# Graph attention, 12 heads: Q and K projected group by group, and stacked by 36 DMAs of 64 KB per batch instead of 12 of 192 KB

## The reference

```python
q = split_heads(x @ Wq + bq); k = split_heads(x @ Wk + bk); v = split_heads(x @ Wv + bv)
scores = q @ k.T / sqrt(32) + beta * adj
scores = where(adj > 0, scores, -9e15)
out = softmax(scores) @ v                 # heads side by side again: 256 x 384
y = layernorm(x + out)                    # over the 384 columns, no affine
```

## Time and profile before

| | us |
|---|---|
| median of 3 runs | 877.06 (875.73 to 879.56) |
| span of the profiled execution | 871.1 |
| PE busy | 748.6 (86%) |
| DVE busy | 643.6 (74%) |
| ACT busy | 632.8 (73%) |
| POOL busy | 420.7 (48%) |
| DMA queue, share of 16 engines | 55.1% |

### The profile page before, as it was taken

How to read it: one execution, slowest core, us unless ns; L and a number is a source line. 1 busy time by engine, 2 the same in 40 slices (tenths; PEclk the granted TensorE clock), 3 DMA queues, 4 the chain that set the end, 5 groups by cost and what they waited for, 6 DMA issues and landing times.

```text
span 871.1 us, 27397 instructions
## 1 busy us (share of the span) xinstructions
PE 748.6 (86%) x6528; PEld 657.1 (75%) x6528; DVE 643.6 (74%) x2487; ACT 632.8 (73%) x2116; POOL 420.7 (48%) x660
## 2 busy tenths in 40 slices
PE   5799998888988888989888989888998888999882
PEld 4678887777887777887777887777787777787761
DVE  3477777777777776877777787777877777787775
ACT  3477877777876777877777877777777777777772
POOL 1312555454555454556454556454456454456453
PEclk9899999999999999999999999999999999999997
DMA  4666444566544566544566545566544566544461
GB/s 151 140 140 140 104 119 117 137 158 155 107 118 114 137 157 156 107 117 116 133 158 157 109 119 116 129 157 158 116 118 114 124 158 157 115 118 113 96 147 36
DMA packets 59226, 111.87 MB, mean 128 GB/s; under 512 B 8704, under 2 KB 34560, under 8 KB 59136
## 3 DMA queue, kind: packets, MB, share of 16 engines
q1 hardware_dynamic: 59136, 111.05, 55.1%
HBM read 22.94 MB, written 12.58 MB: 41 GB/s over the span
## 4 chain that ended last, share of the span: by engine, by line
PE 35%; SPq 33%; DMA 18%; ACT 5%; issue 5%; DVE 3%; ACTq 0%; DVEq 0%
SPq L292 32%; PE j_bank L367 18%; DMA stack<-qk_parts 17%; PE t_bank L396 7%; PE s_bank L381 5%; PE o_bank L412 4%; ACT probs L472 2%; ACT qk_parts L486 2%; DVE qk_parts L567 2%; ACT probs_t L499 1%; PE o_bank L420 1%; DMA beta_col<-in_L_gnn_beta_dram 1%; ACTq L178 0%; PE j_bank L335 0%; DVE w_low L684 0%
## 5 line engine op out<-in xcount | busy, mean ns | idle before, releaser
L472 ACT ACTIVATE probs<-neg_scores,neg_max 128x256 f32<-128x256 f32 x768 | 381.9, 501 | 41.2 <-DVE neg_max L557 37.9
L557 DVE CUSTOM_DVE_ANT_0 neg_scores<-s_bank,bias_sb 128x256 f32<-128x256 f32 x768 | 290.2, 415 | 97.5 <-issue 51.6
L381 PE MATMUL s_bank<-stack 96*128 96x256 f32 x768 | 170.9, 304 | 95.5 <-DMA stack<-qk_parts 95.5
L396 PE MATMUL t_bank<-ident,probs 128*128 128x128 f32 x1536 | 231.4, 272 | 1.8 <-ACT probs L472 1.3
L381 PEld LDWEIGHTS s_bank<-stack 96*128 96x128 f32 x768 | 120.8, 190 | 125.5 <-issue 74.2
L396 PEld LDWEIGHTS t_bank<-ident,probs 128*128 128x128 f32 x1536 | 177.6, 141 | 3.3 <-ACT probs L472 1.8
L486 ACT ACTIVATE qk_parts<-j_bank,qk_bias 128x256 fp32r<-128x256 f32 x192 | 90.7, 473 | 120.6 <-PE j_bank L367 95.6
L577 DVE COPY probs_t<-t_bank 128x512 f32<-128x512 f32 x256 | 175.6, 686 | 1.1 <-PE t_bank L396 1.1
L567 DVE SCALAR_TENSOR_TENSOR qk_parts<-j_bank,qk_bias,qk_parts 128x256 fp32r<-128x256 f32 x192 | 92.4, 481 | 76.4 <-ACT qk_parts L486 76.4
L472 ACT ACTIVATION_READ_ACCUMULATOR probs<-neg_scores,neg_max 128x1 f32 x768 | 146.5, 191 | 0.0
L367 PE MATMUL j_bank<-xt_high,w_high 128*128 128x256 f32 x576 | 116.6, 311 | 6.0 <-ACT w_high L517 5.5
(11 more groups left out here) (59 smaller groups left out, 927.4 us busy)
## 6 DMA issues: line engine op xcount, KB each, us to landing
stack<-qk_parts SPq DMA_DIRECT2D x384, 192.0 KB, 4.0
x_sb<-in_x_dram SPq DMA_DIRECT2D x32, 384.0 KB, 4.9
out_dram<-o_sb SPq DMA_DIRECT2D x31, 384.0 KB, 4.5
adj_sb<-in_adj_dram SPq DMA_DIRECT2D x32, 256.0 KB, 4.8
w_raw<-in_L_gnn_Wq_dram SPq DMA_DIRECT2D x1, 576.0 KB, 4.2
w_raw<-in_L_gnn_Wk_dram SPq DMA_DIRECT2D x1, 576.0 KB, 6.6
w_raw<-in_L_gnn_Wv_dram SPq DMA_DIRECT2D x1, 576.0 KB, 8.2
out_dram<-o_sb SPq DMA_DIRECT2D x2, 192.0 KB, 2.0
```

Source lines behind the costliest of these rows:

```text
L381: mm = pe.matmul(b[:, t * N:(t + 1) * N], stack[0:R, par, 0, j, g, t * P:(t + 1) * P], stack[0:R, par, 1, j, g, :], start=True, stop=True)
L396: mm = pe.transpose(b[:, k * N + t * P:k * N + (t + 1) * P], probs[:, (T * h + t) % (T * NH), k * P:(k + 1) * P], ident[:, :])
L472: nc.scalar.activation(probs[:, slot, :], neg_scores[:, slot, :], ACT.Exp, bias=neg_max[:, par, t, h:h + 1], scale=-1.0, accum_out=row_sum ...
L557: nc.vector.tensor_tensor_reduce(neg_scores[:, (T * h + t) % (T * NH), :], s_bank[h % NS][:, t * N:(t + 1) * N], bias_sb[:, par, t, :], -1 ...
```

## The change

The jobs go Q0 K0 Q1 K1 Q2 K2, so that the two jobs of a group follow each other. `stack_parts` becomes `stack_group`, which moves one group: 12 DMAs of 32 x 2 x 1024 B = 64 KB, each behind a wait for the low part of that group's K job. `stacked` becomes 24 semaphores (parity, group, j) instead of 4, and PE waits at each head for those of that head. In SP's stream group 0 of batch b+1 is issued at the start of batch b, ahead of the loads of x and adj; groups 1 and 2 behind them.

```diff
-    JOB = [(kind, g) for kind in "QK" for g in range(G)] + [("X", 0), ("V", 0), ("X", 1), ("V", 1), ("X", 2)]
+    JOB = [(kind, g) for g in range(G) for kind in "QK"] + [("X", 0), ("V", 0), ("X", 1), ("V", 1), ("X", 2)]
-        stacked = [sem(f"stacked{j}") for j in range(J)]
+        stacked = [[[sem(f"stacked{par}_{g}_{j}") for j in range(J)] for g in range(G)] for par in range(2)]
-            def stack_parts(i, par):
-                multiplied = held(count(i, par, STEPS, -STEPS))
-                wait(sp, low_ready, low_count(i, par, KV - 1))
+            def stack_group(i, par, g):
+                if g == 0:
+                    wait(sp, scores_ready, held(count(i, par, STEPS, -STEPS)))
+                wait(sp, low_ready, low_count(i, par, 2 * g + 1))
                 take_wait(sp, passed_s)
-                wait(sp, scores_ready, multiplied)
                 for j in range(J):
                     for n, (q_part, k_part) in enumerate(PAIRED):
-                        src = qk_parts[HD * j:HD * (j + 1), par, q_part:2 + k_part + 1:2 + k_part - q_part, :, :]
-                        sp.dma_start(stack[HD * n:HD * (n + 1), par, :, j, :, :].bitcast(F32),
-                                     src.bitcast(F32)).then_inc(stacked[j], DMA)
+                        src = qk_parts[HD * j:HD * (j + 1), par, q_part:2 + k_part + 1:2 + k_part - q_part, g, :]
+                        sp.dma_start(stack[HD * n:HD * (n + 1), par, :, j, g, :].bitcast(F32),
+                                     src.bitcast(F32)).then_inc(stacked[par][g][j], DMA)
...
-            stack_parts(0, 0)
+            for g in range(G):
+                stack_group(0, 0, g)
             def batch(i, par):
...
+                if not is_last(i, par):
+                    stack_group(i + par, 1 - par, 0)
                 if not is_tail(i):
...
                     load_adj(i + 1, par)
                 if not is_last(i, par):
-                    stack_parts(i + par, 1 - par)
+                    stack_group(i + par, 1 - par, 1)
+                    stack_group(i + par, 1 - par, 2)
                 if not first:
                     store(i - 1, par)
...
             def scores(i, par, h):
                 g, j = h // J, h % J
-                if g == 0:
-                    wait(pe, stacked[j], count(i, par, PARTS * DMA, PARTS * DMA))
+                wait(pe, stacked[par][g][j], (i + 1) * (PARTS * DMA))
...
             def high(i, par, k):
...
-                    if k == 0:
+                    if q == 0:
                         for j in range(J):
-                            wait(act, stacked[j], count(i, par, PARTS * DMA, -PARTS * DMA))
+                            wait(act, stacked[par][g][j], i * (PARTS * DMA))
```

More of the change, by code:

```diff
@@ L350, in project @@
                 if k < KV:
-                    q, g = k // G, k % G
+                    g, q = k // 2, k % 2
                     pairs = [(wp[:, q, c, g * P:(g + 1) * P], xp[:, par, c, :])
```

## The result

The changed kernel takes 981.54 us in the median (976.61 to 983.27), against 877.07 us for the kernel before: ratio 1.119, with a 95% interval of 1.115 to 1.122. It is slower by 104 us. The forecast was 905 us, slower by 28 us: right in sign, and outside its range of 815 to 935.

A forecast was written before the change was run, and what follows sets the result against it. PE, the busiest engine, was held by waits for stacking DMAs, 2.98 us per batch. Start 53.2, 29 periods of 27.0 (783) and end 63.1 give 899.3, 28.2 over the span; added to 877.06 that is 905 us, range 815 to 935.

The forecast's parts named there:

- the term for the clock: PE behind the late x: granted clock falls in one batch in five, 1.9 us per fall, period 26.6 to 27.0.
- The stack waits go: PE's score matmul: all 2.98 + 0.3 us per batch of waiting for stacking DMAs gone, alone 98 us.
- One 64 KB issue costs 0.64, twelve 7.7: SP's stacking issues: 0.64 us each, so 36 take 23.0 us per batch.
- a cheaper issue: Rival on SP: a 64 KB issue costs 0.43 us, period 24.6, time 826 us; chance 0.22.
- engines held by the number of runs: Rival on the DMA engines: 0.98 us an issue, over 1200 us, or 0.75 and about 1010; chance 0.06.
- SP needs 26.6 us per batch: SP's queue: 23.0 of issues, 3.05 of store and loads, 0.5 of waits.
- x lands 3.65 us after PE wants it: PE at X0: x, issued behind group 0, lands at 386.8 against 383.11; period by this loop 26.5 us.
- the upper bound, 945 us: Clock term on PE: a fall in each batch, period 28.4 us, time 945 us.
- PE without its stack waits needs 22.8 us per batch: PE: period 26.05 less 2.98 of stack waits, less some 0.1 for each of three restarts.
- Start and end: First X0 after the change at 53.2 us with PE at half clock; from the last X0 to the end 63.1 us.
- the first rival: Rival of the cheaper 64 KB issue on SP: X0 of batch 0 at 43.9, 826 us; chance 0.22.
- The limits trade places: Rival: x lands 0.5 us earlier, SP sheds as much, period 26.1, clock holds, 877 us; chance 0.13.

The follow-up runs named there:

- e1: Changed kernel with SP issuing the loads of x and adj ahead of group 0 again, 36 DMAs kept: 873.43 us, ratio 0.995 to the kernel before.
- e3: Changed kernel with groups 1 and 2 stacked in one burst of twelve 128 KB DMAs (24 per batch): 962.24 us, ratio 1.096 to the kernel before.
- e2: Changed kernel with 30 throwaway matmuls on PE ahead of the wait for x: 922.83 us, ratio 1.050 to the kernel before.
- e8: Changed kernel with loads ahead, groups 1 and 2 in one burst, and the loop written out: 766.45 us, ratio 0.873 to the kernel before.
- e5: Changed kernel with the loop written out, no jump back on any engine: 961.78 us, ratio 1.095 to the kernel before.
- e6: Changed kernel with 30 throwaway matmuls ahead of each wait for x and the loop written out: 905.53 us, ratio 1.030 to the kernel before.
- e10: Changed kernel with groups 1 and 2 in one burst, 28 throwaway matmuls and the loop written out: 906.41 us, ratio 1.033 to the kernel before.
- e7: Changed kernel with loads ahead and groups 1 and 2 in one burst, loop kept: 812.70 us, ratio 0.925 to the kernel before.

## Why the prediction was right in sign and too small

The step that failed is the term for the clock: it was to fall in one batch in five, and it fell in every one. A second term was put at nothing without a reason: what DVE does at the jump back, once no stack wait covers it. The rest of the mechanism held.

- *The stack waits go.* Right: none is left.
- *One 64 KB issue costs 0.64, twelve 7.7.* Right: 7.67 to 7.78 in the rows shown. The rivals of a cheaper issue and of engines held by the number of runs are out.
- *SP needs 26.6 us per batch.* Nearly: 26.1 when it is the bound (e1), as store and loads issue in 0.37 to 0.40 each with an undisturbed queue. It was not the bound of the changed kernel (e3).
- *x lands 3.65 us after PE wants it.* Right: 3.84 per batch, landing 3.2 us after its issue. The period that follows, 26.6 with a clock that holds and no jump, is 26.7 in e2. Undoing this one part takes the whole loss back (e1), though there the period is SP's own work, and x is still somewhat late.
- *The granted clock.* Here the term "one batch in five" failed. In the changed kernel it fell behind all 30 waits, and e2 gives the sum: 1.8 us in each batch, against 0.4 taken. That is 1.4 x 29 = 41 us of the 76 that are missing. The price of one fall, 1.9 from the earlier trace rows, was right (the stretch of 30 to 32 us in the earlier trace rows has 0.55 in the mean, where the prediction says 0.50); the upper bound, 945 us, was the better reading. The Trainium skill's rule ("TensorE: Matmul & The Clock Gate", "What's actually happening") said so: the clock follows how busy the array has been, and idling halves it. The trace agrees, with 0.50 to 0.61 behind each wait. The prediction weighed it against the work on both sides of the wait, for which no row stood.
- *PE without its stack waits needs 22.8 us per batch.* Right for PE (e8), wrong for the kernel: it took for granted that nothing hid behind those waits. DVE's gap at each jump back did. The periods give 2.5 us per pass, 1.2 per batch, 35 us in all; together with the clock that is the 76. Written out (e5, e6) only 17 to 20 us of it come back, since the written-out kernels have some half microsecond per batch more on this loop, for a cause that stays open (e10). That e6, with both terms out, measures the 905 us of the forecast is luck: without falls of the clock the forecast was 893.
- *Start and end.* X of batch 2 was issued at 49.5 and forecast at 48.1. From the last X0 to the end it took 66.0 us, forecast 63.1. Both are small beside the 29 periods. Two of the prediction's figures are a little off, without weight in the sum: SP's slack is 12.55 us by its rows, and X0 of the first rival comes out at 43.7.
- *The limits trade places* described e1 (877 forecast, 873 measured), not the changed kernel.

## What to carry to other kernels

Before a step moves ahead in an in-order queue, list what stands behind it and when each of those is wanted; here a load with some 8 us to spare was put behind 7.7 us of issues that had themselves to wait. A wait that goes away uncovers whatever lay beside it, so look for idle time on every engine at the same place, also under the rows marked "issue". And a single long wait of PE can cost more than several short ones of the same sum, since the clock may fall: 2.98 us in three pieces per batch did not bring it down (1.00 from 100 to 850 us of the kernel before), 3.84 in one piece always did, and in e1 single waits from 1.92 us on mostly did.

## What was not expected of the hardware

- Twelve SBUF-to-SBUF DMAs of 64 KB issue at 0.64 us each, the same as twelve of 128 KB (7.77 us in e3), while 192 KB go at 0.95. By the 209 GB/s of the earlier trace rows their bytes would take 0.31, 0.63 and 0.94 us: at 64 KB the issue is the limit, at 192 KB the data, and at 128 KB the two come out alike.
- From its jump back to the first instruction of the next pass DVE's stream takes, in the passes read here, 3.0 us in the changed kernel, 4.2 in the kernel before and 4.4 in e7, and DVE is idle for 2.0 of them in the first and 3.4 in the last; ACT, PE and SP take 0.2 to 0.3. No run shows why, and none tells DVE's jump from those of the others.
- Throwaway matmuls ahead of a wait of about 3.8 us brought 58.7 us, 6% of the kernel, by keeping the granted clock at 1.00.
